# Clearing a table from another queue, and summing two chunks' degrees on VectorE instead of TensorE

## The reference

```python
deg = segment_sum(ones, dst); deg_inv = 1 / max(deg, 1)
def sage(h, W_self, W_neigh, b):
    agg = segment_sum(h[src], dst)
    return h @ W_self + (agg * deg_inv[:, None]) @ W_neigh + b
h = relu(sage(x, W_self0, W_neigh0, b0))
x = layernorm(x + sage(h, W_self1, W_neigh1, b1))
# GCN: self loops added; deg counts src; norm = deg^-0.5[row] * deg^-0.5[col]
x = layernorm(x + segment_sum(norm[:, None] * (x @ W.T + b)[col], row))
```

## Time and profile before

| | |
|---|---|
| median of 3 runs | 851.29 us (848.52 to 852.38) |
| profiled execution | 849.59 us, its span 847.9 us |
| granted TensorE clock, mean | 0.999 |
| PE busy | 830.6 us, 98% |
| DVE, ACT, POOL busy | 461.3, 177.4, 459.1 us |
| DVE's longest wait in mean0 for a fetched self part | 11.5 us |
| ACT's wait for the clears of adj_out in N0 | 13.1 us |

### The profile page before, as it was taken

The page is one execution under the profiler, slowest core; times in us unless marked ns, Lnnn a source line. Parts: engine busy times, 40 slices in busy tenths (PEclk is TensorE's granted clock), DMA queues, the critical chain, the costliest instruction groups (busy, mean ns, idle before and its releaser), DMA issues.

```text
span 847.9 us, 11000 instructions
## 1 busy us (share of the span) xinstructions
PE 830.6 (98%) x4295; PEld 707.9 (83%) x4295; DVE 461.3 (54%) x714; ACT 177.4 (21%) x218; POOL 459.1 (54%) x343
## 2 busy tenths in 40 slices
PE   8999999999999999999999999999999999999996
PEld 6888888888897899788888888778889889988885
DVE  6465568200017565897544677775556435455555
ACT  4111132110111113353123112222222122200000
POOL 5028887787777887885888788788620000000000
PEclk9999999999999999999999999999999999999999
DMA  9977965463776425668876668267877649555551
GB/s 332 380 304 267 350 193 168 125 176 75 213 236 180 122 57 133 249 237 286 298 282 222 243 220 284 62 176 214 240 245 255 223 150 295 189 199 199 198 193 46
DMA packets 99480, 180.52 MB, mean 213 GB/s; under 512 B 15474, under 2 KB 75898, under 8 KB 94048
## 3 DMA queue, kind: packets, MB, share of 16 engines
q1 hardware_dynamic: 60144, 124.17, 44.0%
q10 hardware_dynamic: 26896, 40.65, 13.3%
q0 software_dynamic: 12384, 14.95, 7.6%
HBM read 107.08 MB, written 72.43 MB: 212 GB/s over the span
## 4 chain that ended last, share of the span: by engine, by line
PE 61%; POOL 15%; DMA 9%; issue 8%; DVE 5%; SPq 1%; ACT 1%; POOLq 0%; ACTq 0%; DVEq 0%
PE ps L1572 19%; POOL adj_in L643 14%; PE ps L1429 12%; PE ps L1606 10%; PE ps L1589 9%; PE ps L1515 8%; DMA adj_in<-u 4%; DMA first_rows<-in_L_gnn_W_neigh 1%; DMA spare<-in_x 1%; DMA xin<-s0t_scr 1%; PE ps L1413 1%; DVE u L914 1%; PE ps L1380 1%; SPq L514 1%; DVE sacc L1303 0%
## 5 line engine op out<-in xcount | busy, mean ns | idle before, releaser
L643 POOL DMA_INDIRECT adj_out<-loops,idx_out x160 | 245.2, 1533 | 65.4 <-issue 65.4
L643 POOL DMA_INDIRECT adj_in<-mult,idx_in x160 | 198.1, 1238 | 86.8 <-issue 86.8
L1572 PE MATMUL ps<-u 128*128 128x512 f32 x840 | 190.7, 389 | 1.4 <-DVE u L914 1.4
L1572 PEld LDWEIGHTS ps<-u 128*128 128x128 f32 x840 | 157.6, 188 | 34.2 <-issue 1.6
L1484 PE MATMUL ps<-wx 128*128 128x512 f32 (+1 forms) x576 | 109.4, 351 | 1.3 <-ACT outb L761 1.3
L1484 PEld LDWEIGHTS ps<-wx 128*128 128x128 f32 x576 | 93.9, 189 | 16.9 <-ACT outb L761 1.9
L1429 PE MATMUL ps<-u 128*128 128x512 f32 x432 | 98.2, 389 | 0.0
L1515 PE MATMUL ps<-wx,u 128*128 128x256 f32 (+5 forms) x640 | 94.8, 309 | 1.2 <-DVE ht L1191 1.2
L1589 PE MATMUL ps<-u,panel_tiles 128*128 128x512 f32 (+1 forms) x400 | 93.9, 393 | 1.9 <-DVE u L914 1.9
L1429 PEld LDWEIGHTS ps<-u 128*128 128x128 f32 x432 | 81.0, 188 | 16.8
L1515 PEld LDWEIGHTS ps<-wx,u 128*128 128x128 f32 (+1 forms) x640 | 86.6, 191 | 8.2 <-DVE ht L1191 1.6
(11 more groups left out here) (167 smaller groups left out, 779.8 us busy)
## 6 DMA issues: line engine op xcount, KB each, us to landing
left_scr<-u SPq DMA_DIRECT2D x7, 2560.0 KB, 9.5
u<-left_scr SPq DMA_DIRECT2D x7, 2560.0 KB, 9.6
xt_scr<-wx ACTq DMA_DIRECT2D x10, 1024.0 KB, 9.9
u<-xt_scr SPq DMA_DIRECT2D x10, 1024.0 KB, 5.1
wx<-xt_scr SPq DMA_DIRECT2D x16, 512.0 KB, 4.0
adj_in<-u POOLq DMA_DIRECT2D x4, 1600.0 KB, 25.3
adj_out<-u POOLq DMA_DIRECT2D x4, 1600.0 KB, 16.1
wx<-adj_in SPq DMA_DIRECT2D x5, 1280.0 KB, 7.1
```

The source lines that it names most:

```text
L643: pool.indirect_dma_start(table, bass.IndirectOffsetOnAxis(ap=index[0:EP, j:j + 1], axis=0), counts[0:EP, j:j + 1], None, bounds_check=CEL ...
L1572: ins = nc.tensor.matmul(ps[:, product_bank(g, i, p), :], left_op[n % 2][:, p, k, left, :], right_op[n % 2][:, k, right, :], start=(not on ...
```

## The change

1. **Clears and diagonal of `adj_out`.** They leave POOL. ACT issues five clears of 1,280 KB in the first eighth of the self stage, one after each of steps 2 to 6, ahead of its evictions, and the diagonal after the eighth eviction. The zeros lie in `xin`, which VectorE sets after N0.
2. **First fetches.** SP issues fetches 0 to 3 during self step 20 (behind the clears, whose source they overwrite), and no longer after `load_chunk_1(1)`.
3. **Degrees of chunks 0 and 1.** VectorE sums the panels over their ten row tiles, copies the sum to `colsum`, and PE makes the degrees with a single matmul after block d = 3. Chunks 2 and 3 keep their ten matmuls at the head.
4. **Column via memory.** The small matmuls go in all four chunks. SP stores each chunk's reciprocals to `dinv_scr` at d = 6 and loads the column back after the last. The load of `bias`, whose place `colsum` shares, moves behind it.

```diff
 # SP
+                if i == 20:
+                    sp.wait_ge(adj_out_set, 16 * CLEARS)
+                    for m in range(4):
+                        fetch_self(m)
                 if i == 21:
                     load_chunk_1(0)
...
             for m, (c, d) in enumerate(H_BLOCKS):
                 if m >= 4:
-                    sp.wait_ge(h_sum, fetch_free(m))
-                sp.dma_start(fetch_slot(m)[:, 0:CHUNKS[c][1] * T], s0t_scr[d, :, lines(CHUNKS[c])]).then_inc(s0_in[m % 8], 16)
+                    fetch_self(m)
                 if m in (15, 23):
                     load_chunk_1(2 + m // 17)
+                if d == 6:
+                    t0, n = CHUNKS[c]
+                    sp.wait_ge(dinv_row_done, c + 1)
+                    sp.dma_start(dinv_scr[lines(CHUNKS[c])].rearrange("(a j) -> a j", a=1), dinv_row[0:1, c % 2, 0:n * T]
+                                 ).then_inc(dinv_stored[c % 2], 16)
...
+            sp.dma_start(dinv[:, :], dinv_scr.rearrange("(t p) -> p t", p=P), allow_slow_non_contiguous=True).then_inc(dinv_in, 16)
 # POOL
-                        if (g, c) == (0, RUN // 2) and not general_form:
-                            clear(adj_out, cleared_out)
-                pool.wait_ge(diagonal_set, 32)
+                pool.wait_ge(adj_out_set, 16 * (CLEARS + 2))
 # ACT
+            for a in range(CLEARS):
+                act.wait_ge(*s0_used_by(a + 2))
+                act.dma_start(runs[a, :, :, :], zeros_out.unsqueeze(1).broadcast_to([P, ZERO_TIMES, ZERO_PART])).then_inc(adj_out_set, 16)
...
             for i, (c, d) in enumerate(S0_BLOCKS):
+                if i == KD:
+                    set_diagonal()
 # DVE
                 if d == 0:
+                    if c < 2:
+                        dve.wait_ge(m1_full[c], 16 * n // 2)
+                        nc.vector.tensor_reduce(sacc[:, 0:width].rearrange("p (n j) -> p n j", n=n // 2),
+                                                m1_panels[c][:, :, :, :].bitcast(F32).rearrange("p k n j -> p n j k"), AX_X, ALU.add
+                                                ).then_inc(colsum_done, 1)
+                        dve.wait_ge(colsum_done, 2 * c + 1)
+                        nc.vector.tensor_copy(colsum[:, 0:width], sacc[:, 0:width]).then_inc(colsum_done, 1)
                     dve.wait_ge(deg_full, c + 1)
-                if d == 5:
-                    dve.wait_ge(dcol_full, c + 1)
-                    nc.vector.tensor_copy(dinv[:, t0:t0 + n], ps[:, 6 + c % 2, 0:n]).then_inc(dcol_read, 1)
 # PE
+            def degrees(c, width, exact):
+                pe.wait_ge(s0_free, s0_bank_free(6 + c))
+                pe.wait_ge(colsum_done, 2 * c + 2)
+                bank = ps[:, 6 + c % 2, 0:width]
...
+                    ins = nc.tensor.matmul(bank, ones_r[:, :], colsum[:, 0:width], start=True, stop=True)
+                ins.then_inc(deg_full, 1)
...
-                        if d == 2:
-                            pe.wait_ge(dinv_row_done, c + 1)
-                            for i in range(n):
-                                ins = nc.tensor.matmul(ps[:, 6 + c % 2, i:i + 1], dinv_row[0:1, c % 2, i * T:(i + 1) * T],
-                                                       ones_nt[0:1, 0:1], start=True, stop=True)
-                            ins.then_inc(dcol_full, 1)
+                        if (c, d) in ((0, 3), (1, 3)):
+                            degrees(c, width, exact)
```

More of the change, by code:

```diff
@@ L92, in build @@
         base = -(-nc.sbuf_base // 32) * 32
-        U_AT, WX_AT, R_AT, E_AT, END = (base + n for n in (0, 81920, 163840, 188416, 197120))
+        U_AT, WX_AT, R_AT, E_AT, B_AT, END = (base + n for n in (0, 81920, 163840, 188416, 197120, 201216))
         sb("arena", [P, (END - base) // 4], F32)
@@ L117, in build @@
         ones_r = sb("ones_r", [P, P], F32R)
-        bias = sb("bias", [P, D], F32)
+        bias = at("bias", [P, D], F32, B_AT)
+        colsum = at("colsum", [P, WIDE], F32R, B_AT)
         ident = sb("ident", [P, P], F32)
@@ L526, in _ @@
             load_block(0, 1, 0)
+            for s in range(2):
+                sp.wait_ge(dinv_stored[s], 16 * 2)
+            sp.dma_start(dinv[:, :], dinv_scr.rearrange("(t p) -> p t", p=P), allow_slow_non_contiguous=True).then_inc(dinv_in, 16)
+            sp.wait_ge(deg_full, 4)
+            sp.dma_start(bias[:, :], b1.rearrange("(a d) -> a d", a=1).broadcast_to([P, D])).then_inc(bias_full, 16)
             sp.wait_ge(h_sum, KD * 4)
@@ L631, in _ @@
                 pool.dma_start(where[0:EP, :, :], windows).then_inc(edges_in, 16)
-            def clear(table, done):
-                runs = table.rearrange("(p a j) o -> a p (j o)", a=4, j=ZERO_RUN)
-                for a in range(4):
-                    pool.dma_start(runs[a, :, :], zeros).then_inc(done, 16)
             pool.wait_ge(pool_set, 3)
             pool.wait_ge(w_hi_done, KD)
-            clear(adj_in, cleared_in)
+            runs = adj_in.rearrange("(p a j) o -> a p (j o)", a=4, j=ZERO_RUN)
+            for a in range(4):
+                pool.dma_start(runs[a, :, :], zeros).then_inc(cleared_in, 16)
             def put(table, index, counts, j, done):
@@ L649, in _, with scatter @@
             general = pool.value_load(flag[0:1, 0:1], min_val=0, max_val=1)
-            def scatter(general_form):
-                def diagonal():
-                    pool.wait_ge(cleared_out, 16 * 4)
-                    for i in range(2):
-                        cells = bass.AP(tensor=adj_out.tensor, offset=i * T * (PW + 1), ap=[[PW + 1, T], [PANEL + PW * PW, NT // 2]])
-                        pool.dma_start(cells, ones_nt[:, 0:NT // 2], allow_slow_non_contiguous=True).then_inc(diagonal_set, 16)
+            def scatter():
                 pool.wait_ge(cleared_in, 16 * 4)
@@ L670, in _ @@
             with pool.If(general == 0):
-                scatter(False)
+                scatter()
             with pool.Else():
-                clear(adj_out, cleared_out)
                 pool.dma_start(keys_scr.rearrange("(p g c) -> p g c", g=GROUPS, c=RUN), key[0:EP, :, WINDOW:WINDOW + RUN]
@@ L685, in _ @@
                 pool.wait_ge(prescattered, 16 * EC)
-                scatter(True)
+                scatter()
         @block.scalar
@@ L1265, in _ @@
                 u1_low(1, t0)
+            dve.wait_ge(dinv_in, 16)
             for t in range(NT):
@@ L1498, in mean0 @@
                     pe.wait_ge(m1_full[c], 16 * n // 2)
-                    if c < 2:
-                        pe.wait_ge(s0_free, s0_bank_free(6 + c))
-                    else:
-                        pe.wait_ge(dcol_read, c - 1)
-                    for k in range(NT):
-                        ins = nc.tensor.matmul(ps[:, 6 + c % 2, 0:width].rearrange("p (n j) -> p n j", n=n // 2), typed(ones_r[0:rows(k), :], exact),
-                                               typed(panels[0:rows(k), k, :, :], exact), start=(k == 0), stop=(k == NT - 1))
-                    ins.then_inc(deg_full, 1)
+                    if c >= 2:
+                        pe.wait_ge(deg_read, c - 1)
+                        for k in range(NT):
+                            ins = nc.tensor.matmul(ps[:, 6 + c % 2, 0:width].rearrange("p (n j) -> p n j", n=n // 2),
+                                                   typed(ones_r[0:rows(k), :], exact), typed(panels[0:rows(k), k, :, :], exact),
+                                                   start=(k == 0), stop=(k == NT - 1))
+                        ins.then_inc(deg_full, 1)
                     for d in range(KD):
```

44 lines of the change are left out of this document (31 added, 13 removed).

## The result

The changed kernel takes 853.80 us (median of 9 runs, 852.22 to 856.11), the kernel before 849.97 in 9 runs beside it. The ratio is 1.0049, 95% interval 1.0037 to 1.0062. Forecast were 848.8 us and a range up to 852.5. The profiled execution took 854.73 us with a span of 852.9, against 849.59 and 847.9.

The account below looks back on a forecast made before the run. PE, busy 830.6 of 847.9 us, was taken as the bound. 6.02 - 4.3 + 0.53 + 0.45 - 0.2 = 2.5 us won, so 851.3 - 2.5 = 848.8 us; own range 846.5 to 850.5, with rivals 845.0 to 852.5.

Parts of the forecast that it names:

- the clears in the self stage: Self stage: five clears of 1.31 MB on ACT's queue keep up and cost PE 0.2 us, bounds zero and 4.6.
- TensorE's clock: Wait before chunk 2: PE's clock stays at 1.00 through some 4 us, so no loss is counted.
- What PE no longer does: `mean0` to the end of chunk 1's blocks: fewer degree and column matmuls and no 1.20 us wait, 6.02 us won.
- The wait at chunk 2: `mean0`: chunk 2's panel, loaded behind fetch 15, comes late and PE waits 4.3 us, bounds 3.8 to 5.5.
- rival A: Chunk 2's panel comes in time and PE waits at chunk 3 instead; 4.4 us won, 846.9 us; chance 0.15.
- The column sums: VectorE, chunks 0 and 1: the new strided sums finish before PE needs them and cost zero.
- Rival D: Chunk 1's column sum on VectorE is late, by its ceiling 2 us: 850.8 us; chance 0.05.
- Rival B: Self stage: clears hold up the stores that evictions 4 to 7 wait for; PE loses 4.6 us, 853.2; chance 0.10.
- POOL's 4.1 us: Scatter: with the clears' and diagonal's issue off POOL's queue, puts come 4.1 us earlier.
- no slack at all: Chunk 3 before the change: its panel landed at 321.2 and PE took it at 321.30; no wait was forecast after.
- Rival C: The new wait at chunk 2 lowers PE's clock; 2.5 us lost, 851.3 us; chance 0.13.
- the products and all behind them move as a block: Everything from the products on shifts by the 2.5 us won, with no further gain or loss.

Follow-up runs that it names:

- b3: Kernel before with only the clears and diagonal on ACT's queue in the self stage and the early fetches; degrees and column as before: 853.76 us, ratio 1.0046.
- b4: Changed kernel with the clears moved to the N0 stage on ACT's queue and chunk 2's panel load issued behind fetch 12: 852.89 us, 1.0039 of the kernel before.
- d3: Changed kernel with only chunk 2's panel load moved, issued behind fetch 12 instead of fetch 15: 854.04 us, 1.0048 of the kernel before.
- b1: The changed kernel run again with no edit: 854.12 us, 1.0060 of the kernel before.

## Why the prediction was wrong

Two terms of the sum failed: the clears in the self stage, taken at 0.2 us, and TensorE's clock, taken at nothing. In the profiled execution they cost 3.68 and 4.57 us.

**What PE no longer does: right.** 6.02 us up to chunk 2 was forecast, 6.35 came; the wait of 1.20 went.

**The wait at chunk 2: right,** in place, cause and size (4.3; 4.71), and rival A was rightly made small. The load's issue came 3.35 us later than forecast, with all of PE.

**The column sums: right.** They took 4.83 and 9.45 us, the second 1.85 ns an element, and the second ended at 274.3; VectorE then waited 4.41 us for PE. Rival D was not met. The contiguous price of 1.10 ns would have made the second 5.6 us. The trace agrees with the estimate of 8.9 to 12.8 us from the prices in the Trainium skill ("Vector Engine (DVE) Microarchitecture Reference", "5.2 Measured stream behaviour on trn2").

```profile
264.87 9.45 DVE L1207 TENSOR_REDUCE sacc<-wx 128x512 f32<-128x5120 f32 x1
274.36 0.43 DVE L1211 CAST colsum<-sacc 128x512 fp32r<-128x512 f32 x1
279.19 0.69 DVE L1215 TENSOR_SCALAR dinv_row<-ps 128x512 f32<-128x512 f32 x1 [4.41 <-PE ps L1531]
```

**The clears in the self stage: the first step that failed.** The prediction said 0.2 us; 3.68 came, and b3, which has this part alone, stands at 1.0046. It compared an average need (333 GB/s) with a rate once seen (422 GB/s) and called it enough. They moved 323 GB/s, so they kept up, and that was not the question. What PE waits for is the landing of the four stores of 256 KB behind them, 3.0 us each before and 6.4 to 7.2 now. Rival B had the mechanism, the place and a price of up to 4.6, and got 0.10.

**POOL's 4.1 us: wrong in sign.** "Puts come 4.1 us earlier" counted the instructions taken away and not where the scatter's pause would fall. It came 4.6 us later at put 160. In the changed kernel itself that cost only 0.67 at chunk 3, since PE was late too. But it is why no repair of PE's side helps where the kernel before takes 850 us (b4, d3), and it turned a row that was read ("no slack at all" at chunk 3) into the bound.

**The clock: the second step that failed.** Rival C, given 0.13, happened. It took 1.34 us behind chunk 2's wait (1.11 in the ten matmuls, 0.23 in the blocks) against the 2.5 priced. It did not stay there: "the products and all behind them move as a block" was wrong too, since the clock fell at the start of the products (1.62 us over their 840 matmuls) and in the gather's second chunk (1.61). These two are not in every execution: b1, the same kernel, took 190.7 us for the products and 36.97, not 38.60, for that chunk, at a clock of 1.00. The nine timed executions point the same way: the three with a mean granted clock of 0.995 or more took 852.2 to 852.4 us, the six with less 853.4 to 856.1. The prediction's ground against C was a fall seen only after 5.0 us without a matmul; here it fell within 4.7, in d3 within 2.61, and behind 1.72 and 1.41. The Trainium skill's warning on matmuls that wait for DMAs ("TensorE: Matmul & The Clock Gate", "HAM oscillation — how this bites in real kernels") bears on this. The trace agrees at chunk 2, where PE waited for a DMA (4.71 us, then 0.50); the falls behind 1.72 and 1.41 us came behind waits for VectorE.

The sum with the sizes that came: 6.35 won up to chunk 2, less 3.68 (self stage), 4.71 (wait) and 1.48 (chunk 2 to 3: clock 1.34, wait 0.67, less the column's 0.53) is 3.52 lost at chunk 3. Up to the gather 0.73 comes back: 1.72 because PE's wait ahead of `mean1` shrinks from 1.94 to 0.22, 0.63 in smaller terms, less the clock's 1.62. In the gather's first two chunks 2.31 go, 1.61 of them the clock's. That is 5.10 us between the profiled executions and 3.8 between the medians. The shrunken wait ahead of `mean1` is a gain that the prediction did not have: it is 0 to 0.9 us in every kernel with the new column and 1.93 in b3, which has the old one; no run says which part of the column does it.

## What to carry to other kernels

Work off the busiest engine is won only up to the next thing that arrives on its own schedule: before pricing a saving, list what each later stage waits for and how much slack it has, here a row with none. Traffic added beside a loop that turns on small stores is priced by how much later those stores land, here 6.4 to 7.2 us and not 3.0, and not by the bandwidth left. A wait that opens on the busiest engine is priced with the clock behind it, here 1.2 to 1.6 us for most falls. And instructions taken off a queue do not bring the rest forward by their sum where that queue has a pause of its own in it, as POOL's has.
